# Down product of a quantised feed-forward by one level of Strassen, with seven weight parts a group and y summed on chip in five slabs

## The reference, cut to what matters

```python
Wg = dequant_nf4(gate_q, gate_absmax, (M, HD))      # M = 3584, HD = 1024
Wu = dequant_nf4(up_q, up_absmax, (M, HD))
Wd = dequant_nf4(down_q, down_absmax, (HD, M))
g = jnp.einsum('bsh,mh->bsm', x, Wg)                # x: 4 x 512 rows of 1024
u = jnp.einsum('bsh,mh->bsm', x, Wu)
h = jax.nn.silu(g) * u
return jnp.einsum('bsm,hm->bsh', h, Wd)             # added to x: this is y
```

## Time and profile before

| what | value |
|---|---|
| median of 3 runs | 2702.44 us (2700.54 to 2705.99) |
| span of the profiled execution | 2699.7 us |
| attention and what leads up to the sets | to about 995 us |
| gate and up sets overlap attention's end, then run alone | 1048 to 2052.6 us |
| down product to the end of the span | 2052.6 to 2699.7 us |
| busy share of PE, DVE, ACT, POOL | 91%, 66%, 60%, 57% |

### The profile page before, as it was taken

The page is one execution under the profiler, slowest core; times in us unless marked ns, Lnnn a source line. Parts: engine busy times, 40 slices in busy tenths (PEclk is TensorE's granted clock), DMA queues, the critical chain, the costliest instruction groups (busy, mean ns, idle before and its releaser), DMA issues.

```text
span 2699.7 us, 48588 instructions
## 1 busy us (share of the span) xinstructions
PE 2469.7 (91%) x17864; PEld 1343.9 (50%) x17864; DVE 1786.3 (66%) x3004; ACT 1631.8 (60%) x2998; POOL 1525.4 (57%) x1360
## 2 busy tenths in 40 slices
PE   5899999999985557999999999999997897999999
PEld 3576777777764333444444444444443333444444
DVE  5566678767777766777777777777777666555511
ACT  3466666666665436777777777777775565544400
POOL 2356677777769456777777777777774222222200
PEclk9999999999987568999999999999998998999999
DMA  6243443433232211322222222222325433333232
GB/s 199 81 141 108 119 130 105 121 108 107 80 103 87 77 48 43 90 90 88 89 91 82 83 90 83 89 86 86 93 86 202 139 106 114 105 99 100 93 103 76
DMA packets 225885, 271.11 MB, mean 100 GB/s; under 512 B 37616, under 2 KB 148720, under 8 KB 225648
## 3 DMA queue, kind: packets, MB, share of 16 engines
q1 hardware_dynamic: 225648, 268.00, 31.7%
HBM read 192.81 MB, written 73.40 MB: 99 GB/s over the span
## 4 chain that ended last, share of the span: by engine, by line
PE 49%; DVE 3%; issue 3%; POOL 3%; ACT 2%; DMA 1%; SPq 0%; DVEq 0%; POOLq 0%; ACTq 0%
PE ps L2081 33%; PE ps L2114 16%; POOL xT L455 1%; DVE ps L438 1%; ACT w_l L428 1%; DVE p L438 1%; DVE xT L449 1%; DMA proj<-in_codes 1%; ACT ps L425 1%; POOL xn L1993 0%; POOL q_rows L482 0%; SPq L1940 0%; DMA h_parts<-xn 0%; POOL p L465 0%; POOL x_row L1999 0%
## 5 line engine op out<-in xcount | busy, mean ns | idle before, releaser
L438 DVE TENSOR_TENSOR ps<-ps,w_l 128x512 f32<-128x512 f32 x672 | 443.0, 693 | 283.7 <-ACT w_l L428 157.3
L455 POOL TENSOR_TENSOR xT<-xT,nat 128x512 f32<-128x512 f32 x164 | 208.9, 1274 | 530.5 <-DVE xT L449 530.5
L982 POOL TENSOR_TENSOR arena<-p,arena 128x512 f16<-128x512 f32 x320 | 371.1, 1168 | 225.8 <-ACT arena L1436 225.1
L428 ACT ACTIVATE w_l<-proj 128x512 f32<-128x512 int32 x672 | 397.8, 616 | 9.4 <-DMA proj<-in_codes 9.4
L1428 ACT ACTIVATE p<-ps 128x512 f32<-128x512 f32 x320 | 191.1, 597 | 265.7 <-PE ps L1223 260.8
L1640 DVE TENSOR_REDUCE block_max<-ps 128x4 f32<-128x512 f32 x320 | 219.2, 688 | 182.5 <-PE ps L1194 179.9
L2081 PE MATMUL ps<-arena,q_rows 128*128 128x512 f16 x1344 | 296.4, 380 | 10.5 <-POOL arena L376 10.3
L425 ACT ACTIVATE ps<-proj,small 128x512 f32<-128x512 int32 x336 | 216.9, 677 | 90.2 <-DVE xT L449 87.2
L2339 DVE SCALAR_TENSOR_TENSOR arena<-ps,arena 128x1024 f32<-128x1024 f32 x70 | 84.9, 1221 | 241.2 <-PE ps L2114 230.0
L1164 PE MATMUL ps<-xT,w_h 128*128 128x512 f16 x720 | 222.0, 391 | 10.8 <-POOL arena L1077 10.8
L2081 PEld LDWEIGHTS ps<-arena,q_rows 128*128 128x128 f16 x1344 | 131.8, 98 | 170.7 <-POOL arena L376 10.8
(11 more groups left out here) (246 smaller groups left out, 5951.4 us busy)
## 6 DMA issues: line engine op xcount, KB each, us to landing
proj<-in_codes SPq DMA_DIRECT2D x168, 256.0 KB, 2.6
nat<-in_scales SPq DMA_DIRECT2D x336, 128.0 KB, 2.9
h_parts<-xn SPq DMA_DIRECT2D x112, 256.0 KB, 2.3
nat_parts<-nat SPq DMA_DIRECT2D x48, 256.0 KB, 2.0
...
w_l<-h_parts SPq DMA_DIRECT2D x21, 448.0 KB, 4.1
...
```

The lines of the kernel that those rows point to most:

```text
L428: op = self.nc.scalar.activation(out, self.t.codes[:, t % 2, :], ACT.Copy, scale=slope, bias=intercept)
L438: self.nc.vector.tensor_tensor(other if n == self.LUT - 2 else held, held, other, ALU.max).then_inc(self.lut, 1)
L455: self.nc.gpsimd.tensor_tensor(self.quarter(t), self.quarter(t), self.t.scales[:, t % 2, :], ALU.mult)\
L982: nc.gpsimd.tensor_tensor(p_l[:, n % 2, k, :], p32[:, f % 3, :], p_h[:, n % 2, k, :], ALU.subtract).then_inc(p_low, 1)
```

## The change

The down product too is done by Strassen. A down group is two chunks of the hidden dimension by both halves of the 1024 output columns; the rows are paired across the two halves of the batch. So there are 8 row pairs and, in slabs of 2, 3, 3, 3 and 3 groups, 40 sets. A set has seven products of three matmuls of 128x512 a group: 42 matmuls in the first slab, 63 in the others, 2352 in all where there were 2688.

- The operands h of the seven products are stored as seven tiles (C22, C21+C22, C12-C22, C11, C11+C22, C21-C11, C11+C12). So for each of the 28 up sets there are seven boxes instead of four: five new sums on DVE (`hidden_sum`, both inputs in SBUF), seven instead of four high parts on ACT, low parts on POOL and stores on SP. The three box buffers stay.
- The weights of a down group are made like those of a gate or up step: four tiles, five sums, seven high and seven low parts (before: four high and four low for the same four tiles). During gate and up the last step makes group 0; group 1, the second of slab 0, is made after the last step (`FIRST`), woven with the seven boxes of the last up set. In a slab the twelve tiles of the next one lie on its sets 0 to 6 as 1, 2, 2, 1, 2, 2, 2, and none on set 7.
- Each down set has 2 copies on ACT, `down_differ`, `down_left`, four operations of `down_sums` and `down_right` on DVE (each reads one PSUM bank of 512), and `join`, `add_22`, `add_11` on POOL. Before, each of 80 indices had one DVE addition of 1024.
- h for a set is loaded as one DMA a group or more, into two sets of slots.

The SP, ACT and POOL parts of `half_step` are shown only where their pattern changes; the loops over the down sets on SP and ACT (`draw_tile` of the first tile, both copies, then the other tiles) follow the one shown for POOL.

```diff
     NK = 2 * GROUPS
     WT = 4 * NK
+    SLABS = (2, 3, 3, 3, 3)
...
-        return (t - self.WT) // 2, 2, t % 2
+        i, j = (t - self.WT) // 4, t % 4
+        return 2 * i + (0, 1, 0, 1)[j], 2, (1, 1, 0, 0)[j]
...
+    def parts_free(self, k, m):
+        i, sets = k - self.NK, 2 * self.NK
+        if i <= 0 or i == 2:
+            before = k - 3 if i == 2 else k - 2
+            return 7 * (2 * before + 1) + self.POS[m] + 1
+        if i < 5:
+            return 7 * (sets - 1)
+        return 7 * (sets + 2 * QT * (self.slab_of(max(i - 6, 0)) + 1))
...
+    def draw_tile(self, act, t):
+        k, j = t // 4, t % 4
+        M1, M2, M3, M4, M5, M6, M7 = range(7)
+        after = {0: ((), ()), 1: ((), ()), 2: ((M2, M4), ()), 3: ((M1, M3), (M6, M5, M7))}[j]
+        if k == self.NK + 1 and j == 0:
+            after = ((), (M5, M7))
+        for part in range(2):
+            self.draw(act, t, part)
+            for m in after[part]:
+                self.cut_high(act, k if j else k - 1, m)
+
+    def weigh_tile(self, pool, t):
+        k, j = t // 4, t % 4
+        M1, M2, M3, M4, M5, M6, M7 = range(7)
+        if j == 0:
+            self.scale(pool, t)
+            if k == self.NK + 1:
+                self.cut_low(pool, k - 1, M5)
+                self.cut_low(pool, k - 1, M7)
+        if j == 1:
+            self.scale(pool, t)
+            self.sum_w(pool, k, M2)
+        if j == 2:
+            self.cut_low(pool, k, M2)
+            self.cut_low(pool, k, M4)
+            self.scale(pool, t)
+            self.sum_w(pool, k, M1)
+            self.sum_w(pool, k, M6)
+        if j == 3:
+            self.cut_low(pool, k, M1)
+            self.cut_low(pool, k, M3)
+            self.scale(pool, t)
+            self.sum_w(pool, k, M5)
+            self.cut_low(pool, k, M6)
+            self.sum_w(pool, k, M7)
+            self.cut_low(pool, k, M5)
+            self.cut_low(pool, k, M7)
 
 
...
-    LAST_TILE = WT + 2 * MC
+    ND = ROWS * len(SLABS)
+    LAST_TILE = 4 * feed.NALL
+    DOWN_SCALE = 1.0 / (H_SCALE * F_SCALE)
+
+
+    BOX = (M5, M7, M3, M2, M1, M4, M6)
+    BOX_AT = {m: n for n, m in enumerate(BOX)}
+    NBOX = 7 * NK
+    PLAIN = {M5: C22, M2: C11}
+    H_SUMS = (M7, M3, M1, M4, M6)
...
+
+
+    FIRST = range(4 * (NK + 1), 4 * (NK + SLABS[0]))
...
+    def tiles_in(n):
+        slab, r = n // ROWS, n % ROWS
+        if slab + 1 >= len(SLABS):
             return []
-        lo, hi = 2 * SLAB_AT[s + 1], 2 * SLAB_AT[s + 2]
-        return [WT + lo + n for n in range((hi - lo) * r // RT, (hi - lo) * (r + 1) // RT)]
+        at, count = 4 * (NK + SLAB_AT[slab + 1]), 4 * SLABS[slab + 1]
+        return list(range(at + min(count, count * r // (ROWS - 1)), at + min(count, count * (r + 1) // (ROWS - 1))))
...
+                for slot in range(BOXES):
...
-                sp.wait_ge(product, 7 * NSET)
...
-                .then_inc(h_loaded[idx % H_SLOTS], 16)
+            elif n not in (ROWS, ROWS + 1):
+                sp.wait_ge(product, 7 * (NSET + n - 1))
+            for at in range(SLABS[slab]):
+                for piece, first, count in h_pieces(n, at):
+                    sp.dma_start(piece, dram["h"][r, :, SLAB_AT[slab] + at, 2 * P * first:2 * P * (first + count)])\
+                        .then_inc((h_loaded if slab else first_loaded)[r % 2], 16)
...
-            for n, at in enumerate(tiles_of(k, nb)):
-                for h in stores[2 * n:2 * n + 2]:
-                    store_h(h)
-                if at + 2 < LAST_TILE:
-                    feed.load_tile(sp, at + 2)
+            for h in stores[0:3]:
+                store_h(h)
+            feed.load_tile(sp, tiles_of(k, nb)[0] + 2)
+            for h in stores[3:5]:
+                store_h(h)
+            feed.load_tile(sp, tiles_of(k, nb)[1] + 2)
...
+        def add_22(n):
+            out = y_part(n, C22)
+            pool.wait_ge(left_done, NSET + n + 1)
+            pool.wait_ge(joined, NSET + n + 1)
+            nc.gpsimd.tensor_tensor(out, c32(NSET + n, 0), out, ALU.add).then_inc(y22_added, 1)
+
+        def add_11(n):
+            out = y_part(n, C11)
+            if n < ROWS:
+                pool.wait_ge(y_loaded[y_row(n, 0)], 16)
+            else:
+                pool.wait_ge(right_done, NSET + n - ROWS + 1)
+            pool.wait_ge(right_summed, 2 * (NSET + n) + 2)
+            nc.gpsimd.tensor_tensor(out, c32(NSET + n, 1), out, ALU.add).then_inc(y11_added, 1)
...
-            for n in lows[0:2]:
-                hidden_low(n)
-            if nb == 1 and k + 1 < NK:
+            for b in lows[0:3]:
+                hidden_low(b)
+            if nb == 1:
                 feed.cut_low(pool, k + 1, M2)
                 feed.cut_low(pool, k + 1, M4)
...
-            if nb == 1 and k + 1 < NK:
+            for b in lows[3:5]:
...
-            if nb == 0 and k + 1 < NK:
+            for b in lows[5:7]:
+                hidden_low(b)
+            if nb == 0:
...
-                down_low(at)
+        lows = boxes_of(GROUPS - 1, 1)
+        for n, at in enumerate(FIRST):
+            feed.weigh_tile(pool, at)
+            for b in lows[LATER[n]:LATER[n + 1]]:
+                hidden_low(b)
+        for b in lows[LATER[-1]:]:
+            hidden_low(b)
+        for n in range(ND):
+            tiles = tiles_in(n)
+            if n >= 1:
+                add_11(n - 1)
+            for at in tiles[0:1]:
+                feed.weigh_tile(pool, at)
+            join(NSET + n)
+            add_22(n)
+            for at in tiles[1:]:
+                feed.weigh_tile(pool, at)
+        add_11(ND - 1)
 
     @block.tensor
...
+                pe.wait_ge(*h_ready(n))
+            if m == M4:
+                pe.wait_ge(copied, 2 * s + 1)
+            if m == M5:
+                pe.wait_ge(differed, s + 1)
+            if m == M7:
+                pe.wait_ge(copied, 2 * s + 2)
+            if m == M3:
+                pe.wait_ge(right_summed, 2 * s)
+            if m == M6:
+                pe.wait_ge(left_done, s)
+            out = ps_bank(s, PS_OF[m])
+            for c in range(count):
+                w = feed.parts(NK + SLAB_AT[slab] + c)[m]
+                for a, (h, half) in enumerate(((0, 0), (1, 0), (0, 1))):
+                    mm = nc.tensor.matmul(out, h_part(n, c, m, h), w[:, half, :],
+                                          start=(c == 0 and a == 0 and m in (M1, M2, M3, M6)),
+                                          stop=(c == count - 1 and a == 2), skip_group_check=m in (M4, M5, M7))
+            mm.then_inc(product, 1)
+
+        def down_set(n):
+            pe.wait_ge(right_done, NSET + n - 1)
+            for m in PRODUCTS:
+                down_multiply(n, m)
...
+        def down_copy(n, at):
+            s = NSET + n
+            act.wait_ge(product, 7 * s + (POS[M2], POS[M1])[at] + 1)
+            if n == 0:
+                act.wait_ge(h_done, h_tile(GROUPS - 1, 1, (C11, C22)[at]) + 1)
+            else:
+                act.wait_ge((y11_added, y22_added)[at], n)
+            nc.scalar.activation(c32(s, 1 - at), ps_bank(s, 1 - at), ACT.Copy, scale=DOWN_SCALE).then_inc(copied, 1)
+
...
+        def hidden_high(b):
+            m, i, nb = BOX[b % 7], b // 14, b // 7 % 2
+            if m in PLAIN:
+                act.wait_ge(h_done, h_tile(i, nb, PLAIN[m]) + 1)
+            else:
+                act.wait_ge(h_summed, h_sum_index(b) + 1)
+            if b >= BOXES:
+                act.wait_ge(box_stored[b % BOXES], 16 * (b // BOXES))
+            nc.scalar.activation(h_box[:, b % BOXES, :, 0, :], box_source(b).rearrange("p (q t) -> p q t", t=P),
                                  ACT.Copy).then_inc(h_high, 1)
...
-                hidden_high(n)
-            if nb == 1 and k + 1 < NK:
+            for b in highs[0:3]:
+                hidden_high(b)
+            if nb == 1:
                 feed.cut_high(act, k + 1, M2)
                 feed.cut_high(act, k + 1, M4)
...
+            for b in highs[5:7]:
+                hidden_high(b)
+            if nb == 1:
                 feed.cut_high(act, k + 1, M6)
-            if k + 1 == NK:
-                down_high(tiles[0])
-                for part in range(2):
...
+        def hidden_sum(b):
+            m, at, nb = BOX[b % 7], b // 7, b // 7 % 2
+            one, other, op = H_SUM_OF[m]
+            dve.wait_ge(h_done, 4 * at + max(H_AT[one], H_AT[other]) + 1)
+            g = h_sum_index(b)
+            if g >= 3:
+                dve.wait_ge(h_low, 7 * ((g - 3) // 5) + BOX_AT[H_SUMS[(g - 3) % 5]] + 1)
+            nc.vector.tensor_tensor(t.h_sum[g % 3], h32(nb, one), h32(nb, other), op).then_inc(h_summed, 1)
+
...
             if s >= 2:
                 finish(s - 1)
+            for b in boxes[1:3]:
+                hidden_sum(b)
             look_up(tiles[0])
+            for b in boxes[4:5]:
+                hidden_sum(b)
             if s >= 1:
                 differ(s)
             feed.greater(dve, tiles[1], range(3))
+            for b in boxes[5:6]:
```

(56 more changed lines are left out.)

336 lines of the change are left out of this document (174 added, 162 removed).

## The result

The changed kernel takes 2866.9 us (2862.8 to 2869.6), the kernel before 2701.5 in the same session: a ratio of 1.062 (95% interval 1.059 to 1.064). The forecast was 2796 with a range of 2690 to 2865, so the direction was right, and the time lies 71 us above the forecast and 2 above the range.

The account below looks back on a forecast made before the run. PE was taken as the bound. 2699.7 us + 58 (gate and up) + 36 (down, the -72.6 of matmuls inside) = 2794, with 2.7 more for the median 2796; 8 in 10 range 2690 to 2865.

Parts of the forecast that it names:

- The walked 3.7 us: Gate and up, set 4i+4: queues walked make M5 3.7 us late once a group.
- the term for gate and up: Extra boxes and sums delay gate and up by 4.5 us in each of 13 groups: +58 us, bounds 0 and 104.
- The blocking of sums and POOL: Gate and up: a sum costs 0.69 to 1.23 us; 0.8 us a group taken as falling on the path.
- The clock behind the pause: PE runs below its rate after a pause; 3 us charged, in down slabs 0 to 3 only.
- the down product, +59 instead of +36: Down stage: 683 us against 647.1, so +36 us, with the 72.6 us of saved matmuls inside.
- the 128: Down slabs: the sets of a slab sum to 128 us, where PE needs 109.
- the upper bound: Down stage: at most 720 us, if fourth tiles cost 5 us more each through late PE products.
- C: Down as forecast, gate and up absorb the boxes, M5 not late: 2738 us, chance 0.22.
- B: Gain stays: POOL's chain overlaps the next set, gate and up absorb the boxes, slabs under 115 us: 2624, chance 0.15.
- D: Sums and POOL block each other, box buffers stop ACT: gate and up +104, slabs of 137 us: 2872, chance 0.15.
- A: Both stages as forecast: 2796 us, own range 2755 to 2850, chance 0.48.

Follow-up runs that it names:

- e4: Changed kernel, down stage only: POOL does `add_11` ahead of the fourth tile's last sum and cuts; 2826.1 us, ratio 1.047.
- e2: Changed kernel without the box sums and with only four boxes cut for each up set, seven stores kept; 2754.9 us.
- e17: Changed kernel, second input of each box sum from a PSUM bank (sums wrong), TensorE waiting for the sums only ahead of M1; 2830.1 us, ratio 1.048.
- e14: Changed kernel, box sums moved in between the maxima of the look-ups, both inputs in SBUF, nothing left out; 2917.1 us.
- e13: Changed kernel, box sums moved in between the maxima of the look-ups, second input from a PSUM bank (sums wrong); 2866.3 us.
- e1: Changed kernel without its ten box sums a group; seven boxes still cut and stored; 2824.0 us.
- e3: Changed kernel with only four boxes cut, seven stored, and the ten sums a group made but unused; 2822.1 us.
- e7: Changed kernel, down stage only: every tile's tail behind the next `add_11`, tiles spread 1, 2, 2, 2, 2, 2, 1, 0; 2807.5 us, ratio 1.040.
- e15: Changed kernel with four boxes cut, no sums and seven stores in gate and up, plus e7's down stage; 2706.3 us, ratio 1.0022 against the kernel before.

## Why the prediction was right or wrong

**Right: what would be late, and where.** PE pauses ahead of M5 of the gate set behind an up pair, released by POOL's low part; ACT's copy late by the boxes at the stage change; the copies behind ACT's high parts in set 2 and `add_11` behind the fourth tile's cuts in sets 4 and 6 (e4); the last slab solid. Seven stores cost at most 0.9 us a group (e2), and none of the waits of the down matmuls is put down to a load. The walked 3.7 us stands up once the blocking is taken out, as the sum of two pauses in POOL's chain, 0.5 ahead of M6 and 3.06 ahead of M5: 3.56 us in e17, 3.7 on average. Not foreseen were the pauses ahead of M3 (0.9 to 1.8 us) and M6 (1.4).

**Wrong: the term for gate and up, 4.5 us a group instead of 8.7.** This is the step that failed: +58 us, where the stage grew by 102. It has two failed pieces.
- *The blocking of sums and POOL.* I bounded a sum at 0.69 to 1.23 us by the earlier trace rows and put 0.8 us a group on the path. In the changed kernel it is 2.3 to 2.8 us a group (e17), 3.6 to 3.9 in another order (e14); single sums took up to 1.76. The median of 0.69 in the earlier trace rows was of places where POOL was idle; at the start of set 4i+4 it is not. And POOL's own instructions stretch too, by 0.3 to 0.45 us each, which I did not count, though POOL is the engine on whose chain M5 hangs. It was on record: the first cut of the earlier trace rows, at 1546.04, takes 1.66 us, and I costed cuts at 1.12. The Trainium skill, SBUF — State Buffer, Who interferes with whom, says that both inputs in SBUF make the VectorE instruction contend with GpSimd's reads and one such input does not. The runs agree on both: medians of 1.45 to 1.51 us in e14, at most 0.69 in e13. That one fully blocks the other, as the prediction has it, the rows show only in the sum: the two pairs above take as long as one after the other, but both stretch.
- *The clock behind the pause.* I charged it in the down product and left it out here. The 24 matmuls behind the pause ahead of M5 cost 1.6 us more on average (nothing in two of the 13 groups, 2.7 in the one shown, 3.0 at most).

So 3.7 (the walk) + 2.3 to 2.8 (blocking) + 1.6 (clock) + 0.6 of short gaps makes 8.2 to 8.7, against 8.7. The exact share of each is open to about 1 us, since they overlap.

**Wrong by size: the down product, +59 instead of +36.** The first `add_11` is done 67 us after the last matmul, not 57: M2's low part came at 24, not 21, M1's at 36, not 32, M4 at 59, not 50. The sums of the last boxes meet POOL there too; I have not separated that. A slab takes 133.5 to 136 us; the 128 with its handovers and clock made 132. The difference lies mostly in sets 7 and 0: 9 to 10 + 13.6 us, where I had taken 20.5, as if PE had worked further ahead. 10 + some 3 for each of four slabs makes the 23 us. PE's busy time in the stage is 45 us above 508, where I charged 3 for the clock; how much of that lay on the path no run separates. Two of the recorded sums do not add up: the cycles given for sets 1 to 6 make 107.7 us, not 106, and 5 us more for each of twelve fourth tiles would make the upper bound 743, not 720. Neither changes what came of the forecast.

**The rivals.** C (gate and up absorb the boxes) is out by e1 to e3. B is out: its down slabs under 115 us were not reached even in e7. D gave 2872, with 104 us for gate and up and slabs of 137; that is nearly what came, but for its reason only in part: the blocking is some 37 of the 102 us, and the box buffers hold POOL's cut for M5 by 0.8 us a group, some 10 us, as a bound from the trace that no run tested. (e2 does not test it: it cuts only four boxes into the three buffers.) D with 0.15 and A with 0.48 was the wrong weighting: I had named the row that spoke for D and took its lower end.

**The sum of it.** The change buys 72.6 us of PE time. e15 shows that the down product's own new waits (the first set's chain, 55 us there, and slabs of 123 us for 109 of PE) eat all but 6 us of that even in the better order, and four boxes and seven stores take those and 5 more in gate and up. The boxes add some 100 us to it (e7 against e15: 101), and the order of the tails another 59 (e7).
